# The forward patch transform as four 64x64 matmuls per block instead of two of 64x128

## What is computed

```python
    # layer 0
    x = x + conv3x3(gn(x), sign(weight) * alpha)
    # layer 1, on n = gn(x), P = 8
    h = einsum('oc,bchw->bohw', w_in, n)                 # 64 -> 256 channels
    hp = h in patches of P x P
    f = rfft2(hp) * fft_filt                             # per channel and frequency
    h = patches of irfft2(f) back in place
    h = conv3x3(h, w_dw, depthwise)
    x1, x2 = split(h, 2, axis=1)
    x = x + einsum('oc,bchw->bohw', w_out, gelu(x1) * x2)
```

## Time and profile before

| | |
|---|---|
| median of 3 runs | 5494.31 us (5494.24 to 5495.86) |
| span of the profiled execution | 5491.0 us |
| TensorE matmuls busy | 5361.6 us, 98% |
| TensorE weight loads busy | 3472.6 us, 63% |
| DVE busy | 4649.5 us, 85% |
| ACT busy | 3769.3 us, 69% |
| POOL busy | 4641.4 us, 85% |

### The profile page before, as it was taken

How to read it: one execution, slowest core, us unless ns; L and a number is a source line. 1 busy time by engine, 2 the same in 40 slices (tenths; PEclk the granted TensorE clock), 3 DMA queues, 4 the chain that set the end, 5 groups by cost and what they waited for, 6 DMA issues and landing times.

```text
span 5491.0 us, 174549 instructions
## 1 busy us (share of the span) xinstructions
PE 5361.6 (98%) x75428; PEld 3472.6 (63%) x75428; DVE 4649.5 (85%) x5703; ACT 3769.3 (69%) x4866; POOL 4641.4 (85%) x2727
## 2 busy tenths in 40 slices
PE   5999999999999999999999999999999999999998
PEld 4666666666666666666666666666666666666665
DVE  6889888888888888888888888888889888888876
ACT  3767767676676766767667676676767767676676
POOL 3888888898888988889888888888888888888898
PEclk9999999999999999999999999999999999999999
DMA  2011010110101111011010100101011010110000
GB/s 101 18 49 42 36 43 28 52 39 36 53 22 49 39 38 52 19 53 38 36 52 22 56 32 36 56 36 42 32 49 39 36 42 32 49 42 19 23 21 29
DMA packets 43848, 217.59 MB, mean 40 GB/s; under 512 B 5366, under 2 KB 6104, under 8 KB 36952
## 3 DMA queue, kind: packets, MB, share of 16 engines
q1 hardware_dynamic: 43096, 206.42, 9.8%
HBM read 103.64 MB, written 102.76 MB: 38 GB/s over the span
## 4 chain that ended last, share of the span: by engine, by line
PE 89%; DVE 7%; issue 2%; POOL 0%; ACT 0%; DMA 0%; SPq 0%; DVEq 0%; POOLq 0%; ACTq 0%
PE PS L952 27%; PE PS L970 21%; PE PS L912 14%; PE PS L941 11%; PE PS L984 6%; PE PS L930 6%; PE PS L921 4%; DVE hf L690 3%; DVE v L697 2%; DVE bn L628 1%; DVE g L722 1%; DVE PS L713 0%; DVE PS L706 0%; POOL v_lo L357 0%; DMA alpha_sb<-in_alpha 0%
## 5 line engine op out<-in xcount | busy, mean ns | idle before, releaser
L357 POOL TENSOR_TENSOR v_lo<-v,v_hi 128x1024 f16<-128x1024 f32 (+1 forms) x1792 | 3354.1, 1896 | 496.3 <-ACT v_hi L487 496.3
L697 DVE TENSOR_TENSOR v<-PS,smul 128x1024 f32<-128x1024 f32 (+1 forms) x1792 | 1915.4, 1087 | 425.6 <-PE PS L952 226.5
L487 ACT ACTIVATE v_hi<-v 128x1024 f16<-128x1024 f32 (+1 forms) x1792 | 1652.1, 944 | 706.8 <-DVE v L697 554.0
L952 PE MATMUL PS<-hf,c_nodes 64*128 64x512 f32 (+1 forms) x7168 | 1696.1, 574 | 7.1 <-DVE v L697 3.7
L970 PEld LDWEIGHTS PS<-c_ext,v_hi 128*128 128x128 f16 x14336 | 1128.7, 97 | 477.4 <-issue 289.3
L970 PE MATMUL PS<-c_ext,v_hi 128*128 128x100 f16 (+2 forms) x14336 | 1256.6, 203 | 5.1 <-ACT gel L507 3.4
L970 PE MATMUL PS<-c_ext,v_lo 128*128 128x100 f16 (+2 forms) x14336 | 1248.2, 202 | 0.0
L970 PEld LDWEIGHTS PS<-c_ext,v_lo 128*128 128x128 f16 x14336 | 1116.9, 97 | 1.2
L690 DVE TENSOR_TENSOR hf<-PS,mult 128x1024 f32<-128x1024 f32 (+1 forms) x896 | 954.8, 1086 | 85.1 <-PE PS L941 64.2
L952 PEld LDWEIGHTS PS<-hf,c_nodes 64*128 64x128 f32 x7168 | 570.6, 185 | 473.8 <-issue 125.3
L912 PE MATMUL PS<-S_hi,csign 64*64 64x448 f16 (+2 forms) x8640 | 738.7, 338 | 9.4 <-POOL S_lo L346 9.4
(11 more groups left out here) (74 smaller groups left out, 6243.4 us busy)
## 6 DMA issues: line engine op xcount, KB each, us to landing
out_x<-Xa SPq DMA_DIRECT2D x96, 448.0 KB, 2.5
out_x<-Xb SPq DMA_DIRECT2D x96, 448.0 KB, 2.5
Xa<-in_x SPq DMA_DIRECT2D x8, 2240.0 KB, 9.1
Xb<-in_x SPq DMA_DIRECT2D x8, 2240.0 KB, 8.8
Xa<-in_x SPq DMA_DIRECT2D x8, 1792.0 KB, 6.8
Xb<-in_x SPq DMA_DIRECT2D x8, 1792.0 KB, 7.0
Xa<-in_x SPq DMA_DIRECT2D x8, 1344.0 KB, 5.9
Xb<-in_x SPq DMA_DIRECT2D x8, 1344.0 KB, 6.0
```

What stands on the lines that cost most here:

```text
L357: nc.gpsimd.tensor_tensor(v_lo[:, img, :, k0:k1, :], v32[:, V_BUF[kind(b, s)][img][grp], :, 0:k1 - k0, :], v_hi[:, img, :, k0:k1, :], ALU. ...
L487: nc.scalar.activation(v_hi[:, img, :, k0:k1, :], v32[:, V_BUF[kind(b, s)][img][grp], :, 0:k1 - k0, :], ACT.Copy).then_inc(act_vhi[img], 1)
L697: nc.vector.tensor_tensor(v32[:, V_BUF[kind(b, s)][img][grp], :, 0:k1 - k0, :], PS[:, bank:bank + 2, 0:(k1 - k0) * C2].rearrange("p i (k c ...
L952: last = nc.tensor.matmul(PS[:, bank + side, 0:(k1 - k0) * C2], c_nodes[half, :], hf[half, img, k0:k1, :].rearrange("p k c -> p (k c)"), s ...
```

## The change

Each side's matmul is cut in two by image. The stationary operand becomes 64 pixels x 64 channels, the moving one is the same, and the result goes to the 64 partitions of that image, in the same bank as before. The four matmuls of a block lie on the four quarters of the array, in the order (side 0, image 0), (1, 1), (0, 1), (1, 0).

```diff
             def forward_transform(n, s, bank):
                 pe.wait_ge(act_xT, n * STRIPS + s + 1)
                 for k in range(NBLK):
-                    for side in range(2):
+                    for side, img in ((0, 0), (1, 1), (0, 1), (1, 0)):
                         half = slice(side * P * P, (side + 1) * P * P)
-                        last = nc.tensor.matmul(PS[:, bank + side, k * P * P:(k + 1) * P * P], xT[half, k, :], c_fwd[half, :],
-                                                start=True, stop=True)
+                        last = nc.tensor.matmul(PS[img * C:(img + 1) * C, bank + side, k * P * P:(k + 1) * P * P],
+                                                xT[half, k, img * C:(img + 1) * C], c_fwd[half, :], start=True, stop=True)
                 last.then_inc(pe_xf, 1)
```

## The result

| | before | after |
|---|---|---|
| median of the runs | 5494.65 us (5494.24 to 5495.86) | 5443.94 us (5443.11 to 5445.12) |
| span of the profiled execution | 5491.0 us | 5441.7 us |
| TensorE's matmuls, share of the chain that ended last | 89% | 72% |

The forecast was 5444.

The account below looks back on a forecast made before the run. TensorE leads, but POOL's path holds most plain steps. Saving 0.39 us per strip where TensorE leads gives 3.3 us per image, 50 us in all: 5494.3 - 50 = 5444 us, range 5403 to 5500.

Parts of the forecast that it names:

- The round: Forward transform (line 930): a round of matmuls on four tiles takes 0.058 us instead of 0.111; bounds 0.053 and 0.112.
- The changes of tiling: Between line 930 and line 952 on both sides: 0.09 us each, with line 952's load of 0.107 us uncovered.
- The line's sum of 1.17: Forward transform per strip, tiling changes, loads and rounds included: 1.17 us against 1.56, so 0.39 us less.
- The issue floor: Forward transform: load-matmul pairs no closer than some 28 ns on any tile, round 0.11 us, kernel slower at 5558; chance 0.11.
- Instruction supply: Forward transform: needs 9 ns an instruction, not shown; a halfway limit by supply or reordering window gives 5465 to 5497, chance 0.12.
- What arrives: Whole kernel: savings count only where TensorE is waited for; 3.3 us per image, 50 us in all.
- Convolution steps: Strips with convolution, steps 6 to 12 of an image: TensorE leads, so all 0.39 us arrives in each.
- Step 1: Second strip of an image: DVE waits 0.67 us for TensorE, so the full 0.39 us arrives.
- Step 2: Third strip of an image: waits for TensorE, but POOL's second part ends shortly before, so about 0.2 us arrives.
- Steps 0, 3, 4, 5 and 13: Plain strips of an image: the path over DVE, ACT and POOL leads, so nothing of the 0.39 us arrives.
- Rival 1: Plain steps gain too: all strips but the first give 0.39 us, 87 us in all, 5407; chance 0.09.

## Why the prediction was right

**The round.** Forecast 0.058 us, from the difference of a 128 column and a 64 column load in the earlier trace rows and the 0.005 that the old round had over its load; measured 0.058, from the sum and from the starts of the single matmuls. That column tiles load beside one another was read from two other lines, one fp32 with two tiles, one f16 with four. The run with half of the tiles shows it for this line.

**The changes of tiling.** 0.09 each, read from line 952's neighbours; measured 0.09 ahead of the line and 0.093 behind it. The line's sum of 1.17 came out to the hundredth.

**The issue floor.** Line 970's 28 ns for a piece is not a limit of TensorE as a whole; it can bind within one tile at most, since four tiles start a matmul every 0.058/4 = 14.5 ns. The figure that I cited from the Trainium skill, page "TensorE: Matmul & The Clock Gate", section "Wait — 56ns, not 53.3ns?", about 25 ns from start to start however small the matmul, doesn't hold across tiles in this kernel; the traces decide.

**Instruction supply.** I gave 9 ns an instruction as not shown. It held: the changed kernel needs 8.7 over 0.97 us. But I had put the cliff nowhere. The run with eight tiles found it, as averages over the line, between 8.7 and 5.7, and the changed kernel already touches it: before, the waits of TensorE's matmuls have no line "<- issue", and after there is one. Both waits end 1.2 to 1.3 us after a fetch has landed, and the run with half of the tiles, whose fetches are 611 as before, has none.

```profile
PE PS L970 <- issue: 1.4, 2, 1.0
```

**What arrives.** This is the step that made the forecast. 0.39 per strip over 223 strips would be 87 us; I let it count in the nine steps of an image where TensorE is waited for, and not in the five where POOL is. Convolution steps: 0.39 forecast, 0.386 measured. Step 1: 0.39 and 0.40. Step 2 was sized wrong, 0.20 against 0.30: I took POOL's end of v_lo as fixed against the transform. But POOL's work hangs on the evaluation ahead of the transform, and the change of tiling between the two puts the transform 0.09 us later: POOL starts 822.72 - 820.96 = 1.76 us ahead of the transform before and 816.38 - 814.53 = 1.85 after.

```profile
814.53 6.33 POOL L357 TENSOR_TENSOR v_lo<-v,v_hi 128x1024 f16<-128x1024 f32 x3 [1.09 <-ACT v_hi L487]
```

DVE's second product then follows the transform's start by 2.41 instead of 2.70. Steps 0, 3, 4, 5 and 13 were put at nothing and gave 0.03 on average. So this image saved 3.53 us rather than 3.3. From the first forward transform of the run to the last, the time fell by 52.0 us (from 5332.1 to 5280.2), where I had 50. The span fell only by 49.3, because the part ahead of the first transform was 0.9 us longer and the part behind the last one 1.8; between the profiled executions of all kernels here these two parts lie anywhere from 107.5 to 109.5 and from 49.6 to 54.9 us, and whether the change has a share in that is not shown. The forecast met the median to 0.1 us, and that is luck: the 2 us that I gave too little to the steps were made up by what was lost at the ends and around the span (3.3 us in the forecast, 2.2 measured).

**Rival 1**, all strips gain (5407), falls with the kernel itself at 5444, and comes true once POOL is relieved: 85 us.

## What to carry to other kernels

In this kernel an fp32 matmul with 64 moving columns cost what its weight load cost (a round of 0.112 us with 128 weight columns, 0.058 with 64, 0.056 with 32, where the stream takes over), so cut the weight columns over column tiles until the load is as short as the stream, and stop there: after that each cut only adds instructions. Put the neighbours into the same tiling, since a change cost 0.09 us here and uncovered the load behind it. Before counting a saving, look at the first thing that the next line waits for, step by step: here two paths lay within 0.04 us of one another, and relieving either alone brought nothing in those steps, both together everything.

## What the runs showed of the hardware that I had not expected

- The instructions of TensorE can run out. Single rounds of eight tiles went through at 3.5 ns an instruction, the whole line of 1.28 us took 5.7 each, and 51 times it stopped altogether, up to 3.6 us, until 1.2 to 1.6 us after the next fetch. The fetches grow with the program: 611 before, 660 after, 758 with eight tiles. From 10.01 to 12.42 MB for 37632 instructions more is 64 bytes each, so a fetch of 16 KB brings 256 instructions. Dense lines that the fetches can't keep ahead of are a price of small tiles that no busy time shows. Why a fetch comes late at one strip and not at another, I didn't find.
- fp32 loads and the stream of the same tile overlap: with 64 columns both ways, load and stream of 0.053 each make a round of 0.058, not 0.11.
- Two cuts of the same kind, each in its own line, can have opposite signs alone and add up together (+25, -51, -89 us).
